# One scan over both batch rows from the second channel block on, and diagonal blocks formed once and loaded

## The reference

```
xs, z = jnp.split(layer_norm(x) @ in_w, 2, axis=-1)
xc = silu(depthwise_conv(xs, conv_w) + conv_b)            # 4 taps
delta = softplus(xc @ xd_w @ dtp_w + dtp_b); Bm = xc @ xB_w; Cm = xc @ xC_w
dA = exp(delta[..., None] * A); dBx = (delta * xc)[..., None] * Bm[:, :, None, :]
h = dA_t * h + dBx_t;  y_t = einsum('bdn,bn->bd', h, C_t) # over 257 tokens
out = ((y + D * xc) * silu(z)) @ out_w + x
```

## Time and profile before

| what | value |
|---|---|
| median of 3 runs | 10635.43 us (10620.58 to 10636.7) |
| profiled execution, its own time | 10628.51 us |
| its span | 10626.7 us |
| busy: PE, DVE, ACT, POOL | 8447.0, 8624.7, 5870.0, 7310.6 us |
| mean granted TensorE clock | 0.860 |
| DMA | 730.25 MB, mean 69 GB/s |

### The profile page before, as it was taken

The page is one execution under the profiler, slowest core; times in us unless marked ns, Lnnn a source line. Parts: engine busy times, 40 slices in busy tenths (PEclk is TensorE's granted clock), DMA queues, the critical chain, the costliest instruction groups (busy, mean ns, idle before and its releaser), DMA issues. The chain is left out here.

```text
span 10626.7 us, 153432 instructions
## 1 busy us (share of the span) xinstructions
PE 8447.0 (79%) x42776; PEld 6923.8 (65%) x42776; DVE 8624.7 (81%) x13553; ACT 5870.0 (55%) x8819; POOL 7310.6 (69%) x7270
## 2 busy tenths in 40 slices
PE   6877777777777787777787778777778776999998
PEld 5666666666666666666666666666666664777776
DVE  5998999998999999999999999999999995333332
ACT  4555555555555555555555555555555553444443
POOL 5888888888888888888888888888888884000000
PEclk8888888888888888888888888888888886999999
DMA  2221222222222222212222222222222121000000
GB/s 87 86 71 66 77 86 80 86 80 85 81 80 80 79 86 78 73 67 83 80 86 80 86 80 86 80 81 79 86 80 75 68 78 48 11 8 12 12 8 10
DMA packets 366118, 730.25 MB, mean 69 GB/s; under 512 B 143671, under 2 KB 188891, under 8 KB 365275
## 3 DMA queue, kind: packets, MB, share of 16 engines
q1 hardware_dynamic: 361560, 717.54, 19.3%
q10 hardware_dynamic: 3714, 2.89, 0.1%
HBM read 699.27 MB, written 21.05 MB: 68 GB/s over the span
## 5 line engine op out<-in xcount | busy, mean ns | idle before, releaser
L470 POOL TENSOR_TENSOR bu<-b_all,u_buf 128x514 f32<-128x514 f32 x4096 | 4877.6, 1216 | 167.7 <-DVE h_ps L883 111.6
L883 DVE TENSOR_TENSOR_SCAN h_ps<-decay,bu 128x256 f32<-128x256 f32 x6144 | 4180.0, 736 | 474.1 <-ACT decay L695 286.4
L695 ACT ACTIVATE decay<-delta,neg_a 128x512 f32<-128x512 f32 x4096 | 2808.6, 689 | 3035.2 <-DVE h_ps L883 2159.8
L1129 PE MATMUL y_ps<-ident,ch 128*128 128x128 f32 x16384 | 2628.2, 312 | 766.0 <-DVE ch L899 424.9
L1129 PEld LDWEIGHTS y_ps<-ident,ch 128*128 128x128 f32 x16384 | 2232.9, 162 | 1191.7 <-DVE ch L899 573.3
L479 POOL TENSOR_TENSOR ch<-ch,c_all 128x512 f32<-128x512 f32 x1024 | 1353.4, 1322 | 1241.1 <-DVE ch L883 1240.3
L899 DVE TENSOR_TENSOR ch<-h_ps,c_all 128x512 f32<-128x512 f32 x3072 | 1975.9, 670 | 0.0
L883 DVE TENSOR_TENSOR_SCAN ch<-decay,bu 128x256 f32<-128x256 f32 x2048 | 1503.8, 734 | 22.8 <-PE y_ps L1129 19.9
L1014 PE MATMUL w_ps<-xn,in_w 128*128 128x257 f32 x4096 | 1101.4, 414 | 202.7 <-ACT xn L586 89.6
L1014 PEld LDWEIGHTS w_ps<-xn,in_w 128*128 128x128 f32 x4096 | 809.8, 209 | 368.3 <-issue 87.1
L1472 POOL TENSOR_TENSOR rstd_F<-h_F 128x514 f32<-128x514 f32 x16 | 17.5, 1094 | 1434.9 <-DMA h_F<-h_mid 1434.9
(11 more groups left out here) (247 smaller groups left out, 10807.7 us busy)
## 6 DMA issues: line engine op xcount, KB each, us to landing
b_all<-bc_dram SPq DMA_DIRECT2D x512, 514.0 KB, 8.0
c_all<-bc_dram SPq DMA_DIRECT2D x512, 514.0 KB, 9.0
in_w<-in_L_attn_in_w SPq DMA_DIRECT2D x64, 1024.0 KB, 5.0
x_in<-in_x SPq DMA_DIRECT2D x128, 256.0 KB, 2.6
out_w<-in_L_attn_out_w SPq DMA_DIRECT2D x64, 512.0 KB, 3.9
h_mid<-h_cur SPq DMA_DIRECT2D x32, 257.0 KB, 2.2
h_F<-h_mid SPq DMA_DIRECT2D x16, 514.0 KB, 3.8
out<-o_sb SPq DMA_DIRECT2D x64, 86.0 KB
```

Source lines behind the costliest of these rows:

```text
L470: pool.tensor_tensor(bu[:, s % NBU, :, :].rearrange("p b s -> p (b s)"), b_all[:, n // NU, n % NU, :, :].rearrange("p b s -> p (b s)"), u_ ...
L695: func(decay[:, s % NDP, :].rearrange("p (b t) -> p b t", b=NB), delta[:, c, :, 1:S], ACT.Exp, scale=neg_a[:, k, c, n:n + 1]).then_inc(dec ...
L883: last = dve.tensor_tensor_scan(h[:, cols], decay[:, s % NDP, cols], bu[:, s % NBU, b, 1:], bu[:, s % NBU, b, 0:1], ALU.mult, ALU.add)
L1129: last = pe.matmul(y_ps[:, k, :], ch[:, s % NPR, k * P:(k + 1) * P], ident[:, :], is_transpose=True, start=False, stop=(n == NST - 1 and k ...
```

## The change

1. For c = 1, 2, 3 (s from 16) one scan of 512 covers both rows. For that the decay at the joint (row 1, token 1) must be 0 and bu there must be the full value of h after the first step. POOL writes 1e20 into delta there (`reset_delta`, after ACT has taken exp(-A delta) of token 1 with its true value in `joint_gain`), so that the decay comes out as 0. It forms gain x B(0) x u(0) + B(1) x u(1) for all 16 states and both rows (`joint_part_0`, `joint_part_1`), writes it over B's token 1 in b_all, and sets u's token 1 to 1 (`set_joint`), so that b times u gives it without another operation. B's own token 1 is kept in b_keep. The first row starts in the same way. b times u is then 128x512, read from the second element of each row on. c = 0 stays as it was. A is held at least 1e-17.
2. The h_ps slot follows the count of states that DVE multiplies, not s.
3. The diagonal blocks of all four Mamba blocks are formed once in the lead-in, in the room of c_all and b_all, stored to DRAM, and loaded by each pass with DMAs of 256 KB: one for skip_diag (now for all four c, double) and four for the convolution. They stand on SP between the weights and bring_bc. In the lead-in load_x stands behind the first of them.

```diff
+            def store_diagonals(job):
+                sp.wait_ge(diag_built, job + 1)
+                sp.dma_start(diag_dram[job].rearrange("c p n -> p c n"), conv_stage[:, job, :, :, :].rearrange("p c k n -> p c (k n)")
+                             ).then_inc(diag_stored, 16)
+                sp.dma_start(skip_dram[job], skip_stage[:, job, :, :].rearrange("p c n -> p (c n)")).then_inc(diag_stored, 16)
+            def load_diag(g, jj, c):
+                if c < 2:
+                    if positive(job_count(g, jj - 1, CI, CI)):
+                        sp.wait_ge(delta_ready, job_count(g, jj - 1, CI, CI))
+                else:
+                    sp.wait_ge(full_of(f"cv{c - 2}", g, jj), nth(f"cv{c - 2}", g, jj))
+                sp.dma_start(conv_diag[:, c % 2, :, :].rearrange("p k n -> p (k n)"), diag_dram[jj % 4, c]
+                             ).then_inc(diag_loaded[c % 2], 16)
...
                 load_weights(0)
+                for job in range(4):
+                    store_diagonals(job)
+                sp.wait_ge(diag_stored, 4 * 2 * 16)
+                load_skip(0, 0)
+                load_diag(0, 0, 0)
+                load_diag(0, 0, 1)
                 load_x(0, 0)
+                load_diag(0, 0, 2)
+                load_diag(0, 0, 3)
...
+            def reset_delta(g, jj, c):
+                pool.wait_ge(gain_ready, job_count(g, jj, CI - 1, c))
+                pool.wait_ge(u_ready, job_count(g, jj, CI, c + 1))
+                pool.tensor_tensor(delta[:, c, 1, 1:2], reset_root[:, :], reset_root[:, :], ALU.mult).then_inc(delta_reset, 1)
+            def joint_part_0(g, jj, c):
+                if c == 1:
+                    pool.tensor_copy(b_keep[:, :, :], at_token(1))
+                pool.tensor_tensor(carried[:, :, :], gain[:, c, :, :], at_token(0), ALU.mult).then_inc(joint_parts, 1)
+            def joint_part_1(g, jj, c):
+                u = [u_buf[:, c % 2, :, t].unsqueeze(2).to_broadcast([P, NB, NST]) for t in (0, 1)]
+                pool.wait_ge(u_ready, job_count(g, jj, CI, c + 1))
+                pool.wait_ge(joint_parts, job_count(g, jj, CI - 1, c))
+                pool.tensor_tensor(carried[:, :, :], carried[:, :, :], u[0], ALU.mult)
+                pool.tensor_tensor(added[:, :, :], b_keep[:, :, :], u[1], ALU.mult).then_inc(joint_sums, 1)
+            def set_joint(g, jj, c):
+                pool.wait_ge(joint_sums, job_count(g, jj, CI - 1, c))
+                pool.wait_ge(b_done, job_count(g, jj, STATES, NST * c))
+                pool.tensor_tensor(at_token(1), carried[:, :, :], added[:, :, :], ALU.add)
+                pool.memset(u_buf[:, c % 2, :, 1:2], 1.0).then_inc(joints_set, 1)
...
+                if n == 0 and c > 0:
+                    pool.wait_ge(joints_set, job_count(g, jj, CI - 1, c))
...
+                if c > 0:
+                    pool.tensor_tensor(bu[:, s % NBU, 0:NB * L].rearrange("p (b t) -> p b t", b=NB),
+                                       b_all[:, n // NU, n % NU, :, 1:], u_buf[:, c % 2, :, 1:], ALU.mult).then_inc(b_done, 1)
+                    return
...
+            def joint_gain(g, jj, c):
+                k = BLOCK_OF_JOB[jj % 4]
+                act.wait_ge(delta_ready, job_count(g, jj, CI, c + 1))
+                for b in range(NB):
+                    last = func(gain[:, c, b, :], neg_a[:, k, c, :], ACT.Exp, scale=delta[:, c, b, 1:2])
+                last.then_inc(gain_ready, 1)
...
+                if s >= NST:
+                    dve.tensor_tensor_scan(h, decay[:, s % NDP, :], bu[:, s % NBU, 0:NB * L], 0.0, ALU.mult, ALU.add
+                                           ).then_inc(scan_done, 1)
+                    return
```

More of the change, by code:

```diff
@@ L239, in mamba_phase @@
         xn_ready = sem("xn_ready")
-        diag_ready = sem("diag_ready")
+        diag_built = sem("diag_built")
+        diag_stored = sem("diag_stored")
+        diag_loaded = [sem(f"diag_loaded{i}") for i in range(2)]
+        skip_loaded = sem("skip_loaded")
         bc_stored = sem("bc_stored")
@@ L395, in period @@
                         load_x(g, 4)
+                    load_skip(g, jj + 1)
+                    for c in range(CI):
+                        load_diag(g, jj + 1, c)
                     bring_bc(g, jj + 1)
@@ L415, in _, with build_diagonals @@
                                pattern=[[-1, P]], channel_multiplier=1).then_inc(ident_set, 1)
[L417 to L442, removed]
+            def build_diagonals(job):
+                k = BLOCK_OF_JOB[job]
+                for c in range(CI):
+                    pool.tensor_tensor(conv_stage[:, job, c, :, :], ident[:, :].unsqueeze(1).to_broadcast([P, KW, P]),
+                                       conv_w[:, k, c, :].unsqueeze(2).to_broadcast([P, KW, P]), ALU.mult)
+                pool.tensor_tensor(skip_stage[:, job, :, :], ident[:, :].unsqueeze(1).to_broadcast([P, CI, P]),
+                                   d_skip[:, k, :].unsqueeze(2).to_broadcast([P, CI, P]), ALU.mult).then_inc(diag_built, 1)
             def step_size(g, jj, c):
@@ L501, in lead_in @@
                 pool.wait_ge(ident_set, 2)
-                for c in range(CI):
-                    conv_weights(0, 0, c)
-                skip_weights(0, 0, 0)
+                pool.wait_ge(zeros_set, 6)
+                for job in range(4):
+                    build_diagonals(job)
                 step_size(0, 0, 0)
@@ L519, in period @@
                         delta_x(g, jj, s // NST + 1)
-                    if s % NST == 12 and not (last and s > 3 * NST):
-                        skip_weights(g, jj, s // NST + 1)
+                    if s % NST == 12 and s < 3 * NST:
+                        reset_delta(g, jj, s // NST + 1)
                     if s == 3 * NST + 6:
@@ L868, in step_size, with h_slot @@
                                              op0=ALU.add, op1=ALU.min).then_inc(sp_sums, 1)
+            def h_slot(s):
+                return len([v for v in range(s) if v not in POOL_C]) % NU
             def scan(g, jj, s, b):
@@ L953, in period @@
                     s = NU * u
-                    scan(g, jj, s, 0)
-                    scan(g, jj, s, 1)
+                    for b in range(NB if s < NST else 1):
+                        scan(g, jj, s, b)
                     if u - 1 in y_at(jj):
@@ L962, in period @@
                     scan(g, jj, s + 1, 0)
-                    if s + 1 in POOL_C:
+                    if s + 1 in POOL_C and s < NST:
                         c_times_h(g, jj, s)
@@ L966, in period @@
                     else:
-                        scan(g, jj, s + 1, 1)
+                        if s < NST:
+                            scan(g, jj, s + 1, 1)
                         c_times_h(g, jj, s)
-                        c_times_h(g, jj, s + 1)
+                        if s + 1 not in POOL_C:
+                            c_times_h(g, jj, s + 1)
                     if size:
```

86 lines of the change are left out of this document (60 added, 26 removed).

## The result

| what | before | after |
|---|---|---|
| median | 10636.07 us (10620.58 to 10637.4) | 10381.99 us (10372.69 to 10389.18) |
| profiled execution, its span | 10628.51, 10626.7 | 10389.18, 10387.4 |
| busy: PE, DVE, ACT, POOL | 8447.0, 8624.7, 5870.0, 7310.6 | 8344.1, 8087.7, 5899.2, 7059.5 |

The ratio is 0.9765 (95% interval 0.9753 to 0.9777): 254 us faster. The forecast was 10330, the range 10140 to 10560. DVE does 537 us less work, and the span is 239 us shorter: more than half of what DVE saved came back as waits.

What follows compares the result with a forecast made beforehand. DVE, busy 92% of the 64 passes, was taken as the bound. Terms -507 + 31 + 119 + 42 + 10 = -305 us from 10628, plus 7, gave near 10330 us; range 10140 to 10560.

Steps and rivals of the forecast that it cites:

- One scan for two, -507: DVE, states 16 to 63: two scans of 256 become one of 512, saving 0.165 us on 3072 pairs: -507 us.
- Rival (a): Joined scans on DVE save only the call, 0.112 us a pair: -344 us, so 10490 us; chance 0.12.
- Lead-in, +31: Before the passes: POOL forms 20 blocks, stored before the tokens' input is loaded; +31 us (25 to 50), once.
- Borders, +119: POOL where one c ends and the next begins: +154 us, less 35 given back; +119 us (0 to 400).
- Its walk: POOL and DVE followed from scan 25 to state 32: POOL needs 11.0 us; 0.8 us put at each border.
- Rival (d): The borders cost nothing, with POOL's small steps at 0.2 us or more lead: near 10130 us; chance 0.10.
- b times u, 0: POOL's product, now read as two rows of 256 starting one element in, keeps its mean price: 0 us.
- (b): POOL pays 1.27 us for every b times u, about +160 us: 10490 us; chance 0.13.
- (c): POOL becomes the bound through b times u in states 16 to 63: slower, near 11400 us; chance 0.06.
- ScalarE, +42: At each silu DVE finishes its two states 0.33 us sooner and waits that much more, 128 times: +42 us.
- six small gains a pass: About 0.2 us each: they fit, since DVE leaves never less than 1.71 us for a decay of 0.69.
- TensorE, +10: Rises from 77 to about 79% of the stage; eight ch slots still hide it; late y costs +10 us.

Runs made afterwards that it cites:

- e1: The changed kernel, with the joined scan taking its start 0.0 through a pointer instead of a constant: 10408.27 us, ratio 0.9792.
- e3: The joined scans alone against the kernel before: POOL forms all diagonal blocks in each pass and the lead-in is the old one; 10431.25 us, ratio 0.9814.
- e2: The changed kernel, with the tokens' input loaded ahead of the stores of the diagonal blocks on SP: 10354.71 us, ratio 0.9745.
- e7: The changed kernel with taps 2 and 3 of the convolution left out: 10230.17 us, ratio 0.9627.
- e8: The kernel before, with taps 2 and 3 of the convolution left out: 10603.95 us, ratio 0.9975.
- e11: e2 with DVE's multiplication of the c = 1 output one unit later, at state 40 instead of 38: 10351.74 us, ratio 0.9728.
- e5: The changed kernel with its silus as Identity on 8 elements and the preload of the next table left out: 10306.44 us, ratio 0.9697.

## Why the prediction was right, and which terms were not

The sum was -305 us and the result is -254, inside the forecast's own range (10230 to 10430). The traces give the sum that the prediction should have had, in DVE's time, for the 64 passes: -538 busy time, +144 waits for decays, +78 waits for TensorE (y's 85 and some small ones, less 20 for y_ps that went), +36 for the logarithm, -4 for POOL, some +24 of small waits. That is -260; with 23 of lead-in it is the 239 us between the spans, to 2 us. Against it, the terms:

1. **One scan for two, -507: right.** 1.12 us from start to start, 1222 ns (1.21 predicted), pointer 59 ns in e1, 1.18 us from start to start with it. Rival (a), only the call, falls. The rule of VectorE: DVE Perf Modes in the Trainium skill (errata) that stood beside it would have given 184 or 384 us for DVE, and that section says itself that its 58 cycles come out too low; DVE's busy time fell by 537. The joined scans alone (e3) took 492 us off it, the loaded blocks another 40 (e2), which no term had.
2. **Lead-in, +31: 23.4.** POOL's product of ident and weights takes 1.04 us, under the 1.09 to 1.32 of its neighbours, and the last store took 4.4 us.
3. **Borders, +119: the term that failed most.** What it gave back for the blocks was right: 35 was put, and 41 went at state 44. Its small operations were about right. Its walk was not. It put 0.8 us at each of 192 borders, 154 us, and the trace has 30 us, all at the third border of a pass (states 47 and 48). At the first, DVE comes from c = 0, whose scans are still the old ones, and the walk had them at the new pace. At the second, DVE comes from its wait behind a silu (state 22 or 26), and b times u of state 32 is done 1.5 us (median) before its scan starts. The net for POOL is -4, not +119. Rival (d), that the borders cost nothing, was nearer on the borders and 250 us off in time, because of the next two terms.
4. **b times u, 0: right.** 1191 ns at 128x512 where it was 1216 at 128x514. Rivals (b) and (c) fall: POOL is busy 82% of the stretch.
5. **ScalarE, +42: mis-sized.** The waits for decays rose by 144. The place was right and the size half: the silus have 88 of it, 0.5 to 0.7 us each instead of 0.33. The other part is what the term ruled out: that the "six small gains a pass" fit in 1.71 us. Behind a product taken out and behind the normalization DVE now waits 60 us, and it waits 161 times for the decay of a ch state, where it waited 13 times. The wait for the logarithm, 36, was in no term.
6. **TensorE, +10: mis-sized.** 78 by the waits, up to 120 by the pair e7 and e8. I looked at its share of the stage, 79%, and at eight slots of ch. The y of c = 1 passes through TensorE and ScalarE before DVE can use it, and DVE now comes to it earlier: its wait alone rose from 21 to 78 us.

So the number was right by luck in part: errors cancelled. DVE's waits for POOL came out 123 us under the forecast, DVE's own saving 31 and the lead-in 8 better; the waits for ScalarE's decays 102, for TensorE 68 and those in no term some 60 worse. With short silus the change brings 364 and with two taps 374. Whether these add up was not tried.

Of the signs named, the 1.21 us scan came true, the first scan came at 144 and not 152, waits for decays at 433 and not 330, waits for POOL at 138 and not 250, a pass at 133 us and not 132, POOL busy 7.06 ms and not 7.3.

**The version that beats both** is e2 (10354.71 us), or e11 (10351.74), which can't be told from it: the tokens' input goes first on SP. By the whole times it is barely apart from the changed kernel; the first scan, 23 us earlier, is the surer sign.

## What to carry to other kernels

Here DVE bounded the stage at 92% busy, and a saving on it was worth less than its size: the joined scans alone brought 40% of it, the last 163 us 18%. What took it back stood at few places of a pass, behind a silu and at one y, on engines busy 58% and 77% of the stage. Their shares did not show it; a count of DVE's waits state by state did. Before such a change, walk DVE up to each of these places at its new pace, from the wait before it, and not from a free start: that walk went wrong here for POOL.

Preparation that costs little beside slow work (POOL's block forming, 17 us) had a price beside fast work (73 us, each within some 20), so the order in which two changes are tried decides how each looks.

## What the runs showed of the hardware

- A start value read by pointer costs a scan 59 ns, at 512 elements (1281 against 1222).
- DVE's product-and-sum on 128x514 with both inputs in SBUF has no single duration. The softplus line for even and odd c, min, median and max in ns, in the changed kernel:

```profile
L953 DVE SCALAR_TENSOR_TENSOR diag_store<-diag_store x128: 674/713/1508, 136.2 to 8557.2; 128x514 f32<-128x514 f32 x128
L953 DVE SCALAR_TENSOR_TENSOR sq<-sq x128: 837/1680/1724, 139.1 to 8561.7; 128x514 f32<-128x514 f32 x128
```

  In the tail, where POOL is idle, a product of that size with both inputs in SBUF takes 720:

```profile
L1766 DVE TENSOR_TENSOR sq_A<-sq_A 128x514 f32<-128x514 f32 x16 | 11.5, 720 | 19.5 <-ACT sq_A L1617 19.5
```

  GPSIMD Engine Reference in the Trainium skill (Specifications) says that GpSimd shares its SBUF interfaces with VectorE, with contention where a VectorE instruction has two SBUF inputs. The rows fit that, and c times h, whose h is in PSUM, stays at 671 ns; no run here took POOL away from these lines alone.
- The table load takes 1283 ns in every row; ScalarE: Activation LUTs in the Trainium skill (What ACT_TABLE_LOAD costs) states the same and adds a drain of 1380 ns for every switch of set. In this trace the silu starts 0.02 us after its load ends (4021.53 + 1.28 against 4022.83 in the earlier trace rows), and all idle time before the 510 loads of e5 is 9 us, so the traces have no such drain on either side of a load.
